# A decoder layer on one core of Trainium2: the places of all pieces in the hand-written order of five engines set anew

## What is computed

```python
def layernorm(x): return (x - mean(x)) / sqrt(var(x) + 1e-5)

# 1: relu-squared attention against fixed keys and values, 4 heads of 64
xn = layernorm(x) * ln_g + ln_b
p  = square(relu(einsum('bhtd,sd->bhts', heads(xn), k)))      # k: 1024 x 64
x1 = layernorm(x + x + einsum('bhts,sd->bhtd', p, v))

# 2: cross attention with the context, 16 heads of 16, a bias from frac
D  = clip(frac[:, None, :] - frac[:, :, None], -0.2, 0.2)
a  = gamma * Q @ K.T / 4 + delta * (alpha_pos * max(D, 0) + alpha_neg * min(D, 0))
x2 = layernorm(x1 + softmax(a) @ V @ Wo.T + bo)

# 3: feed forward with a low-rank term of the one expert that the gate picks
e  = argmax(x2 @ gate_W.T + gate_b)
h  = relu(x2 @ wi_W.T + wi_b + x2 @ lora_A[e].T @ lora_B[e].T)
out = layernorm(x2 + h @ wo_W.T + wo_b)
```

## Time and profile before

| | us |
|---|---|
| median of 3 runs (lowest, highest) | 865.58 (864.62, 867.97) |
| the profiled execution | 868.24 |
| its span (first to last instruction) | 866.4 |
| PE busy | 824.3 (95%) |
| DVE busy | 720.1 (83%) |
| ACT busy | 704.0 (81%) |
| POOL busy | 581.2 (67%) |
| mean granted clock of PE | 0.987 |

### The profile page before, as it was taken

How to read it: one execution, slowest core, us unless ns; L and a number is a source line. 1 busy time by engine, 2 the same in 40 slices (tenths; PEclk the granted TensorE clock), 3 DMA queues, 4 the chain that set the end, 5 groups by cost and what they waited for, 6 DMA issues and landing times.

```text
span 866.4 us, 23427 instructions
## 1 busy us (share of the span) xinstructions
PE 824.3 (95%) x8444; PEld 594.3 (69%) x8444; DVE 720.1 (83%) x2148; ACT 704.0 (81%) x1930; POOL 581.2 (67%) x754
## 2 busy tenths in 40 slices
PE   7889899999999999999999999999999999999896
PEld 6545556767777676767767676676768667667686
DVE  5887988887888888888888888888888887889854
ACT  3658998897888989798897979888898988888841
POOL 5677878675777868586786768678776867543511
PEclk9998999999999999999999999999999999999899
DMA  7233222222131213223122312313231321323100
GB/s 170 99 65 69 50 56 44 42 40 56 44 62 44 56 38 57 45 52 67 44 57 44 68 26 60 59 45 61 50 63 20 64 55 32 62 45 56 32 14 25
DMA packets 38149, 46.32 MB, mean 53 GB/s; under 512 B 10417, under 2 KB 27313, under 8 KB 38034
## 3 DMA queue, kind: packets, MB, share of 16 engines
q1 hardware_dynamic: 38034, 44.82, 26.0%
HBM read 15.42 MB, written 4.19 MB: 23 GB/s over the span
## 4 chain that ended last, share of the span: by engine, by line
PE 84%; DVE 5%; ACT 4%; issue 2%; POOL 2%; SPq 1%; DMA 1%; POOLq 0%; DVEq 0%; ACTq 0%
PE bank L308 12%; PE bank L503 12%; PE bank L295 11%; PE bank L256 10%; PE bank L421 8%; PE bank L435 7%; PE bank L405 4%; PE bank L381 4%; PE bank L362 2%; PE bank L328 2%; PE bank L342 2%; PE bank L513 2%; PE bank L387 2%; ACT P L711 1%; DVE T L939 1%
## 5 line engine op out<-in xcount | busy, mean ns | idle before, releaser
L1165 POOL TENSOR_TENSOR R<-R 128x512 f32<-128x512 f32 x208 | 220.4, 1063 | 74.8 <-ACT R L655 74.4
L711 ACT ACTIVATE P<-T,NM 128x256 f32<-128x256 f32 x512 | 256.9, 512 | 13.0 <-DVE NM L939 12.9
L1183 POOL TENSOR_SCALAR U<-DP,alph 128x512 f32<-128x512 f32 x256 | 188.1, 736 | 108.5 <-DVE NM L939 72.8
L930 DVE SCALAR_TENSOR_TENSOR bank<-DN,alph,bank 128x512 f32<-128x512 f32 x256 | 180.2, 749 | 47.3 <-PE bank L405 47.1
L939 DVE CUSTOM_DVE_ANT_0 T<-bank,U 128x256 f32<-128x256 f32 x512 | 185.9, 419 | 2.4 <-POOL U L1183 1.3
L655 ACT ACTIVATE R<-bank 128x512 f32<-128x512 f32 x248 | 134.0, 597 | 30.9 <-PE bank L295 29.2
L633 ACT ACTIVATE STG<-bank 128x512 f32<-128x512 f32 x256 | 138.5, 596 | 13.9 <-PE bank L421 12.5
L308 PE MATMUL bank<-R,VS 128*32 128x512 f32 x992 | 120.6, 602 | 6.2 <-DVE R L884 3.8
L295 PE MATMUL bank<-SK,KH 64*128 64x512 f32 x480 | 107.4, 443 | 5.7 <-ACT XO L655 2.4
L711 ACT ACTIVATION_READ_ACCUMULATOR P<-T,NM 128x1 f32 x512 | 103.6, 202 | 0.0
L421 PEld LDWEIGHTS bank<-ident,P 64*128 64x128 f32 x2048 | 77.1, 140 | 36.4 <-issue 27.7
(11 more groups left out here) (180 smaller groups left out, 1826.2 us busy)
## 6 DMA issues: line engine op xcount, KB each, us to landing
QS<-QK SPq DMA_DIRECT2D x384, 64.0 KB, 2.3
XG<-in_x SPq DMA_DIRECT2D x16, 256.0 KB, 3.0
CT<-in_ctxT SPq DMA_DIRECT2D x16, 256.0 KB, 2.9
out<-XO SPq DMA_DIRECT2D x15, 256.0 KB, 2.5
FK<-in_frac SPq DMA_DIRECT2D x16, 128.0 KB, 3.2
STG<-in_wiT SPq DMA_DIRECT2D x2, 512.0 KB, 5.5
STG<-in_woT SPq DMA_DIRECT2D x2, 512.0 KB, 4.3
STG<-in_kT SPq DMA_DIRECT2D x2, 256.0 KB, 4.1
```

The lines of the kernel that those rows point to most:

```text
L711: eng.activation(P[n % NP][:, cs], T[n % NT][:, cs], ACT.Exp, bias=NM[:, n % 8, q:q + 1], scale=-1.0, accum_out=SU[n // 16 % 2][:, q, seat ...
L930: eng.scalar_tensor_tensor(out=L[:, :], in0=dn[:, :], scalar=alph[:, 16 + h:17 + h], in1=L[:, :], op0=ALU.mult, op1=ALU.add).then_inc(s_t1, 1)
L1165: eng.tensor_tensor(r, r, r, ALU.mult).then_inc(s_sqp, 1)
L1183: eng.tensor_scalar(U[n % NU][:, :], dp[:, :], alph[:, h:h + 1], 0.0, ALU.mult, ALU.add).then_inc(s_u, 1)
```

## The change

Every place is a new number. No piece is added, none is left out, and none changes its engine; inside the pieces there is one new line, a wait of `differences` for the small loads. The numbers of identity products behind `filler` are the same, 76 before and after. Sorted by place, most of each engine's sequence in the steady part is unchanged too. What differs there (batch b's period; units are numbered from 0):

- PE: `turn` 1 is ahead of `otT`, not behind it.
- ACT: `rb` of b-1 is ahead of the first `relu`, `aoh` ahead of `exps` 3 (was behind 4), `x2` ahead of `exps` 8 (was behind it).
- DVE: `biased` 7 is ahead of `centred a` of b+3, not behind it; then come, as before, `gating` of b-1, `differences` of b+1 and `ull` of b-1. Further `ao` ahead of `biased` 2, `cl` ahead of `y2`, `stats a` ahead of `biased` 5, `rc` ahead of a square, the squares a place or two later.
- POOL: `rsqrt d` after `positive` 0 (was after 13, for an earlier batch's output), `rsqrt a` ahead of `positive` 12, `plus` of X2b after `rsqrt b`, `plus` of X1b after `positive` 14, `rsqrt c` one unit earlier. `gain` follows the square of unit 11 and precedes `positive` 0 of the next batch, as before.
- SP: `load_x` and `load_f` behind the fourth `restack`; the store of XO is that of one batch later at the same spot.

In the last batch its own `late` shifts put `centred a` ahead of `biased` 7 as before. At the start: `xnT(0)` is behind the first 15 identity products (was behind 18), four more stand ahead of the first `scores`; on SP the context's load is first and FK's is behind Wq's; on DVE the low halves of Wv and Wk and the statistics of batch 1 are ahead of the second half of KL; on ACT the fourth `relu` unit is ahead of the projection of K; on POOL `gain(1)` is ahead of the third square; `bias_o` on PE is ahead of the sixth `scores`; 2 + 4 identity products stand between the first `logits` and `vp`; the normalisation of output batch 0 is after `biased` 2 of batch 3 (was between `differences` and `ull` of the period before), and `rsqrt d` of it after `positive` 6. In the end: one identity product moves a half batch earlier, `logits` 7 of the last batch is ahead of `turn` 5, `gs` of batch 14 ahead of a copy, the first `ffn_in` of batch 14 ahead of `turn` 7.

The diff, cut to the lines that set these:

```diff
@@ PE
-                if g == -2405:
+                if g == -4785:
                     pe.wait_ge(s_id, 1)
                     filler(15, pV)
...
-                if g == -605:
+                if g == -61:
                     pe.wait_ge(s_id, 1)
                     filler(6, pV)
...
-                for b, u in due(g, -11, 8, 74, early=35, late=5):
+                for b, u in due(g, -13, 8, 75, early=30):
                     logits(8 * b + u)
...
-                for b, u in due(g, 114, 8, 78, early=42, late=7):
+                for b, u in due(g, 119, 8, 78, early=32, late=5):
                     turn(8 * b + u)
...
-                for b, _ in due(g, -462, early=-136, late=6):
+                for b, _ in due(g, -443, early=-43, late=-29):
                     otT(b)
...
-                for b, _ in due(g, 1273, late=351):
+                for b, _ in due(g, 1276, early=-1, late=298):
                     uT(b)
-                for b, u in due(g, -1158, 8, 73, early=-189, late=2):
+                for b, u in due(g, -1153, 8, 73, early=-228, late=4):
                     scores(b, u)
-                if g == -2074:
+                if g == -4491:
                     xnT(0)
@@ DVE
             def differences(b):
                 dve.wait_ge(d_f, 16 * b + 16)
+                dve.wait_ge(d_small, 160)
                 dve.wait_ge(s_t1, 16 * b)
...
-                for b, _ in due(g, -71, early=-958, late=113):
+                for b, _ in due(g, -41, early=-849):
                     differences(b)
...
-                for b, u in due(g, 56, 8, 68, early=24, late=5):
+                for b, u in due(g, 11, 8, 77, early=42, late=-5):
                     biased(8 * b + u)
...
-                for b, _ in due(g, -1400, start=2, late=-5):
+                for b, _ in due(g, -1356, start=2, late=-60):
                     dve.wait_ge(s_xnT, b)
                     centred("a", b, XN, XG[b % 2], s_x0)
...
-                for b, _ in due(g, 2095, early=-189, late=1142):
+                for b, _ in due(g, 2047, early=84, late=1323):
                     dve.wait_ge(d_o, 16 * b)
...
-                for b, _ in due(g, 1197, early=-5, late=985):
+                for b, _ in due(g, 1205, early=4, late=817):
                     gating(b)
-                for b, _ in due(g, 1334, early=-97, late=1074):
+                for b, _ in due(g, 1282, early=-36, late=1037):
                     ull(b)
@@ POOL
-                if g == -982:
+                if g == -1055:
                     gain(1)
-                for b, _ in due(g, -1279, start=2, late=11):
+                for b, _ in due(g, -1250, start=2, late=2):
                     gain(b)
...
-                for b, _ in due(g, 1815, early=6, late=1805):
+                for b, _ in due(g, 1995, early=204, late=1468):
                     rsqrt("d", b)
...
-                for b, u in due(g, -1049, 16, 37, early=-214, late=8):
+                for b, u in due(g, -1030, 16, 38, early=-173, late=3):
                     if not on_dve(b, u):
                         square(b, u)
@@ SP
-                if g == -3042:
+                if g == -4725:
                     load_c(0)
-                if g == -2711:
+                if g == -407:
                     load_f(0)
...
-                for b, u in due(g, 1005, 4, 116, early=-53, late=209):
+                for b, u in due(g, 872, 4, 94, early=-40, late=-5):
                     restack(4 * b + u)
```

More of the change, by code:

```diff
@@ L584, in _ @@
                     ffn_in(b, u)
-                for b, u in due(g, 1310, 4, 29, early=-16, late=370):
+                for b, u in due(g, 1311, 4, 30, early=-15, late=379):
                     low_rank(b, u)
-                for b, u in due(g, 1426, 8, 24, early=-1, late=2067):
+                for b, u in due(g, 1433, 8, 23, early=1, late=1467):
                     ffn_out(b, u)
-                for b, _ in due(g, 761, early=-53, late=-6):
+                for b, _ in due(g, 763, early=-59, late=-53):
@@ L620, in _ @@
                     scores(b, u)
-                if g == -2074:
+                if g == -4491:
                     xnT(0)
-                if g == -807:
+                if g == -839:
                     xnT(1)
-                for b, _ in due(g, -1225, start=2, late=-31):
+                for b, _ in due(g, -1236, start=2, late=-16):
                     xnT(b)
@@ L767, in _ @@
             for g in GRID:
-                for b, u in due(g, 1297, 4, 36, early=-7, late=476):
+                for b, u in due(g, 1297, 4, 36, early=-15, late=936):
                     ih(b, u)
-                for b, _ in due(g, -376, early=903, late=-9):
+                for b, _ in due(g, -372, early=987, late=-18):
                     x1(b)
-                for b, u in due(g, 28, 16, 38, early=27, late=6):
+                for b, u in due(g, 30, 16, 38, early=24, late=-9):
                     exps(16 * b + u)
-                if g == -4999:
+                if g == -2944:
@@ L775, in _ @@
                     skh(0)
-                if g == -1030:
+                if g == -1400:
                     skh(1)
-                for b, _ in due(g, -1260, start=2, late=-7):
+                for b, _ in due(g, -1259, start=2, late=-11):
                     skh(b)
-                for b, _ in due(g, -491, early=-275, late=2):
+                for b, _ in due(g, -489, early=-673, late=-8):
                     heads_out(b)
-                for b, u in due(g, 119, 8, 76, early=49, late=33):
+                for b, u in due(g, 121, 8, 75, early=37, late=44):
@@ L783, in _ @@
                     turned(16 * b + 2 * u)
                     turned(16 * b + 2 * u + 1)
-                for b, _ in due(g, 820, early=-13, late=449):
+                for b, _ in due(g, 773, early=-15, late=118):
                     aoh(b)
-                for b, _ in due(g, 774, early=-64, late=97):
+                for b, _ in due(g, 765, early=-68):
                     rb(b)
-                for b, _ in due(g, 977, early=101, late=-53):
+                for b, _ in due(g, 966, early=94, late=35):
@@ L830, in _ @@
                     gs(b)
-                for b, _ in due(g, 1260, early=-27, late=398):
+                for b, _ in due(g, 1270, early=-59, late=191):
                     ulh(b)
-                for b, u in due(g, -1155, 8, 72, early=-433, late=2):
+                for b, u in due(g, -1154, 8, 72, early=-820, late=1):
                     relu(b, 2 * u)
@@ L1081, in _ @@
                         centred("d", b, XO, X2b, s_xo)
-                if g == -1505:
+                if g == -1569:
                     dve.wait_ge(d_small, 160)
@@ L1118, in _ @@
                     cl(b)
-                for b, _ in due(g, -243, early=-51, late=65):
+                for b, _ in due(g, -222, early=-69, late=30):
                     low("x1T", b, X1L, X1H, s_x1h, s_x1l)
-                for b, _ in due(g, -202, early=-1223, late=33):
+                for b, _ in due(g, -191, early=-1239, late=29):
                     projected("kp", b, 2, 2, s_kh, s_kl)
-                for b, _ in due(g, -179, early=-2, late=35):
+                for b, _ in due(g, -189, early=46, late=50):
@@ L1130, in _ @@
                     ull(b)
-                for b, u in due(g, -1121, 16, 40, early=-569, late=-28):
+                for b, u in due(g, -1126, 16, 41, early=-585, late=-14):
                     if on_dve(b, u):
@@ L1227, in _ @@
                     plus(X1b[b % 2], X1, boB, s_x1b)
-                for b, _ in due(g, 1517, early=-164, late=315):
+                for b, _ in due(g, 1636, early=23, late=-147):
                     pool.wait_ge(s_x2, 2 * b + 2)
```

204 lines of the change are left out of this document (102 added, 102 removed).

## The result

The changed kernel took 879.35 us (median of 4, 878.09 to 880.38), the kernel before 865.32 (median of 4): ratio 1.0156 (95% interval 1.0130 to 1.0181), 14.0 us slower, where 5.2 were forecast. The direction was right, the time inside the range, the size too small by a factor of two to nearly three.

The account below looks back on a forecast made before the run. The prediction took TensorE (PE), busy 824.3 of 866.4 us, as the bound. On the median 865.58 it summed 12.7 + 3.4 - 2.9 - 5 - 1 - 2 = +5.2 to 870.8, say 871 us; range 855 to 883.

Parts of the forecast that it names:

- No products left out, no pairing: Whole kernel: identity products equal (76), half-height loops already there, so "two products left out" and "two heads together" cost nothing.
- The swap on DVE: Periods 1 to 11: `centred a` behind `biased` 7 makes `gain` collide with gating, delaying `uT`; +12.7 us.
- Rival 1: Gating in the steady periods isn't held up, leaving gains and at most 1.7 us of loss: 856 us; chance 0.3.
- The clock, +3.4: Steady periods: idle pieces of 1.1 and 0.46 us close together lower PE's clock in two of 11 periods; +3.4 us.
- Rival 2: Same collision, clock falling in every period, front gaining nothing: 900 us, with half of both 882; chance 0.05.
- The tail: Last batches: `biased` 7 starts earlier, most of GS's wait goes, first `ffn_in` no longer waits for `turn` 7; -2 us.
- needed 8 us later, so nothing: SP's queue: `restack` 2 and 3, ahead of load_x and load_f, behind XO's store, 0.4 to 0.5 us issue each; no cost.
- The front, -5: Start: PE's 2.42 us wait at 22.81 goes, first logits some 2.5 earlier, 2.5 more at 65.03; -5 us.
- periods 0 and 1, -1: Periods 0 and 1: turn ahead of `otT`, rc ahead of a square; -1 us, between -3 and 0.
- the wait at 65.03: Front: six identity products fill PE's 1.76 us wait; with 3.4 us lost to the clock, 2.5 of 5.2 taken as gain.
- XO of batch 0, -2.9: Stall at 197.80: moving XO after `biased` 2 of the next period cuts PE's 1.67 us idle and the clock drop; -2.9 us.
- PE's own sequence is the same but for `turn` 1 ... I cost it at nothing: Steady period on PE: `turn` 1 now ahead of `otT`, both ready by then; no cost.

Follow-up runs that it names:

- e3: The changed kernel with `centred a` put back ahead of `biased` 7 in periods 1 to 11: 863.88 us, ratio 0.9970 to the kernel before.
- e1: The kernel before with one number changed, `centred a` behind `biased` 7 in periods 1 to 11: 883.6 us, ratio 1.0196.
- e2: The kernel before with `centred a` behind `biased` 7 and POOL's `gain` behind `positive` 0 of the next batch: 874.1 us, ratio 1.0083.
- e8: As e1, with `gain` as two one-input tensor_scalar instructions, ln_g and ln_b left out of the input's normalisation: 871.35 us, one run.
- e11: The changed kernel, unchanged, measured again in a later session: 877.59 us, ratio 1.0133 to the kernel before.
- e4: The kernel before up to the logits of batch 12, then the changed kernel's sequence: 866.84 us, ratio 1.0006.
- e14: e13 up to the logits of batch 12, then the sequence of the kernel before: 865.45 us, ratio 0.9988.
- e7: The kernel before with only the fourth relu unit of batch 0 ahead of the projection of K on ACT: 867.14 us, ratio 1.0000.
- e5: e3's sequence for the first two and a half batches, XO of batch 0 included, then that of the kernel before: 864.62 us, ratio 0.9956.
- e6: The kernel before with XO of batch 0 moved behind `biased` 2 of batch 3, and its store moved too: 864.88 us, ratio 0.9976.
- e12: e3 with `stats a` of batch b+3 behind `biased` 5 on DVE: 868.51 us, ratio 1.0030.
- e13: e3 with `stats a` of batch b+3 behind the low half of x1T, as in the kernel before: 867.7 us, ratio 1.0005.
- e9: e3 with `ffn_in` 0 of batch b-1 ahead of `turn` 7 in batches 1 to 13: 885.07 us, ratio 1.0208.
- e10: The kernel before, unchanged, run again for a second profile: 865.86 us.

## Why the prediction was right or wrong

The time lies in the range, but the forecast rests on two halves, and one of them failed. The loss by the swap with its clock was put at 12.7 + 3.4 = 16.1 us and is 14 to 16. The gains were put at 2.9 + 5 + 1 + 2 = 10.9 us, and e3, which has all of them without the swap, gives 2.6 (1.6 to 3.7).

- **No products left out, no pairing: right.** The counts on PE are the same, 8444.
- **The swap on DVE: right, in mechanism and size.** `gain` at 445.55 forecast, 445.57 found; end of L981 446.86 and 446.87; U2 written by 448.6, and 448.55 found; `uT` 1.14 late, and 1.05 found; eleven periods. e1 makes it with one number, e2 takes it away by moving `gain`, e3 by undoing the number. Rival 1 (gating not held up) is out. The rule of the Trainium skill ("SBUF — State Buffer", "Who interferes with whom"), that the two forms exclude each other for the whole instruction, holds to 0.03 us for both L981 and L986; the row for L985 that the prediction lacked is there now. It does not hold in e8, where POOL's instruction has one SBUF input: L980 took 0.41 us there and ended 0.88 us before POOL's did.
- **The clock, +3.4: of the right size or too large.** One drop in the eleven periods in the first profile of the changed kernel (0.68 from 552 to 556 us), none in e11; two were taken. Rival 2, the clock falling in every period, is out.
- **The tail, "-2, between -3.5 and 0": the step that failed.** It is +2.7 by the marks of the two pairs of profiles, +1.0 by those of all sixteen, and between nothing and +2.2 by the times of e4 and e14: 2 to 5 us from the forecast, by every measure outside its bounds or at their edge. Of the steps that I looked at, one went as forecast (`biased` 7 follows DVE's work without a gap) and one went half way (the wait for GS fell from 1.18 to 0.56); no `ffn_in` waits, but none waited in the kernel before either. What I had not followed is where `logits` 0 of batch 15 meets its six restack DMAs. The prediction priced the restacks at "needed 8 us later, so nothing". In the steady part 8.2 us lie between the first issue and the `logits` (437.01 to 445.20 in the kernel before). In the last batch the projection of Q stands closer ahead of the logits: 5.6 us before, and in the changed kernel PE is ready 4.5 us after the first issue (793.34 to 797.86) and waits 2.19 more.
- **The front, -5, and periods 0 and 1, -1: by the marks right in sum, not in its parts; by the times too large.** The marks give -5.4 without the wait at `uT` 0, and both signs came true (`otT` of batch 0 before 35 us, clock 1.00 from 60 to 80). But by the granted clock in windows of 4 us, 3.5 of these 5.4 us are drops up to `uT` 0, which cost 5.2 and 3.4 us in the two profiles of the kernel before and 1.7 and 0 in those of the changed one; 1.9 are left for the order itself. The forecast had 2.5 for the clock and the wait at 65.03 together, and 3.5 for the rest of the order. Over all profiles the new front is 4.0 us shorter (`uT` 0 at 138.6 on average against 142.6, the wait at `uT` 0 taken off), without e7, which has the old front but for the relu and reaches 138.4. By the times, e5 less e6 leaves 1.7 us, with wide intervals. That the marks met the forecast was in part luck.
- **XO of batch 0, -2.9: right in mechanism, sized 0.8 too large** (e6: -2.1, 1.0 to 3.1). In the changed kernel XO waits 1.30 us for `rsqrt d`, as foreseen.
- **"PE's own sequence is the same but for `turn` 1 ... I cost it at nothing", and nothing for the other edits of the period: wrong by 0.12 us a period**, 1.3 us, as e3 shows with the swap undone. Which edit it is, e12 and e13 left open.
- **Base.** The sum was set on the median, 865.6, and later sessions found 866.0 to 867.1; no part of the error.

The range held the time because its upper end was made of the loss's bounds, not because the small gains were seen.

## What to carry to other kernels

Where an order is moved, ask of each small instruction on the path to the bound engine what the *other* engine that shares SBUF will run beside it: here 0.17 us became 1.1 twice, on account of a neighbour's place and not of its own. A place for a piece is judged with the piece that it lets start (`centred a` lets `gain` start), and a fix that moves that one must be checked for the next reader behind it (e2, e7, e9, e12 and e13 each traded a wait for another). And the last batch has its own margins: a restack whose first DMA is issued 8.2 us before its use in the steady part, and of which the last has landed 5.6 to 7.0 us after that, had 4.5 us there. A mark in a profile is one execution: read from two profiles, the end seemed to cost 2.7 us, and from sixteen 1.0.

The best versions of these runs are e5 (ratio 0.9956), e3 (0.9970) and e6 (0.9976), all a little faster than the kernel before and not told apart by their intervals; e3 differs from the changed kernel in one place, e6 from the kernel before in two.

## What was not expected of the hardware

A drop of TensorE's clock to its lower level costs about the same each time: by the granted clock of the windows (one minus the clock, times the length, over neighbouring windows of 4 us), 1.7 us of full speed or twice that. The same kernel shows drops at different places from one execution to the next (first profile of before: at 65, 105, 200, 815 us; e10: at 20, 65, 195, 815). That makes a part of the spread of 4 us between runs of one kernel: of the 17 runs of the kernel before beside e3, the seven with a mean granted clock of 0.988 or less average 867.7 us, the four with 0.991 or more 865.4. It is not all: the profile of e12 has no drop up to 784 us, and its twelve runs lie 7.0 us apart.

The six DMAs of a restack are issued 0.6 to 0.7 us apart in each of these profiles, but the last one's landing is not the same: `logits` 0 of batch 15 start 5.6 us after the first issue in both profiles of the kernel before (784.94 to 790.51), without a wait, and 6.4 us after it in e7 (778.61 to 785.04), with a wait of 0.95 and the same sequence of the end. In the changed kernel it is 6.7 us (793.34 to 800.05), and in e13, which differs from it by two DVE pieces of the steady part only, 5.6 (780.94 to 786.50). Why, was not tried.
